# Perceiver block on one core: shifted-copy clearings, key powers, filter taps and the third level's masks in another order on VectorE and GpSimd

## The reference, cut to what matters

```python
q = _short_conv(hidden_states @ Wq.T, conv_q)          # 4 lags, then silu; the same for k and v_direct
beta = sigmoid(hidden_states @ Wb.T)
local_s, local_m, local_l = _fir(v_direct, fir_s), _fir(v_direct, fir_m), _fir(v_direct, fir_l)   # 3, 15, 63 lags
# delta rule: q, k normalised (k / sqrt(sum k*k)); kb = k * beta
A = where(tri_strict, -(kb @ k.T), 0);  T = solve_triangular(eye - A, eye)
...
probs = softmax(gate logits) * (1 - 5 eps) + eps
o = probs0*local_s + probs1*local_m + probs2*local_l + probs3*delta_out + probs4*v_direct
o = rmsnorm(o) @ Wo.T
```

## Time and profile before

| | us |
|---|---|
| median of 3 runs | 430.43 |
| lowest and highest of the runs | 428.21, 432.83 |
| the profiled execution, its own time | 433.92 |
| its span in the trace | 432.1 |
| mean granted TensorE clock of that execution | 0.987 of full |

### The profile page before, as it was taken

The page is one execution under the profiler, slowest core; times in us unless marked ns, Lnnn a source line. Parts: engine busy times, 40 slices in busy tenths (PEclk is TensorE's granted clock), DMA queues, the critical chain, the costliest instruction groups (busy, mean ns, idle before and its releaser), DMA issues.

```text
span 432.1 us, 8272 instructions
## 1 busy us (share of the span) xinstructions
PE 408.7 (95%) x3210; PEld 290.3 (67%) x3210; DVE 320.0 (74%) x583; ACT 189.0 (44%) x252; POOL 82.8 (19%) x81
## 2 busy tenths in 40 slices
PE   6999999999988989999999999999996999999994
PEld 5953458644434746687764688888884888888873
DVE  4742536697799999897598675855549699999966
ACT  1113322578652211023350445324426788887731
POOL 1100001000023800228741000368100000000065
PEclk9999999999999999999999999999997999999998
DMA  7999987947313540056000200287599889999645
GB/s 261 432 428 422 430 378 274 301 110 196 119 39 109 150 94 8 4 209 281 3 0 2 99 2 0 67 322 217 88 423 367 325 312 371 396 383 397 222 125 192
DMA packets 18227, 92.42 MB, mean 214 GB/s; under 512 B 3457, under 2 KB 5265, under 8 KB 11153
## 3 DMA queue, kind: packets, MB, share of 16 engines
q1 hardware_dynamic: 15168, 78.82, 49.6%
q10 hardware_dynamic: 1488, 8.93, 5.9%
q0 software_dynamic: 1536, 4.20, 3.0%
HBM read 82.25 MB, written 12.08 MB: 218 GB/s over the span
## 4 chain that ended last, share of the span: by engine, by line
PE 64%; DVE 13%; DMA 7%; POOL 6%; issue 5%; SPq 3%; ACT 1%; POOLq 0%; ACTq 0%; DVEq 0%
PE bank L984 22%; PE bank L797 8%; PE bank L721 5%; PE bank L747 5%; PE bank L626 3%; PE bank L603 3%; PE bank L650 3%; PE bank L576 2%; DVE part L1613 2%; POOL xs L522 2%; DMA early<-wffn_in 2%; SPq L376 2%; POOL info L526 2%; DVE ring L1613 2%; PE bank L771 2%
## 5 line engine op out<-in xcount | busy, mean ns | idle before, releaser
L1613 DVE SCALAR_TENSOR_TENSOR part<-ring,cols,part 128x504 f32<-128x504 f32 (+13 forms) x64 | 42.7, 725 | 0.2
L747 PE MATMUL bank<-xnT,ring 128*128 128x512 f32 (+1 forms) x96 | 37.7, 544 | 0.7 <-ACT xnT L1144 0.7
L797 PE MATMUL bank<-ring 64*64 64x64 f32 (+1 forms) x960 | 36.0, 224 | 2.4 <-POOL ring L484 1.3
L797 PEld LDWEIGHTS bank<-ring 64*64 64x64 f32 x960 | 31.8, 134 | 9.3 <-issue 5.7
L475 POOL TENSOR_TENSOR small<-small 128x1 f32<-128x1 f32 (+2 forms) x12 | 12.1, 1006 | 128.6 <-DVE small L1489 67.7
L721 PE MATMUL bank<-early,ring 128*32 128x512 f32 (+15 forms) x512 | 32.9, 396 | 0.5 <-DVE early L1632 0.5
L1613 DVE SCALAR_TENSOR_TENSOR ring<-bank,cols,ring 128x504 f32<-128x504 f32 (+2 forms) x36 | 26.3, 732 | 5.0 <-ACT ring L1207 4.1
L747 PEld LDWEIGHTS bank<-xnT,ring 128*128 128x128 f32 x96 | 17.6, 190 | 17.1 <-issue 15.3
L484 POOL TENSOR_TENSOR ring<-ring,consts 128x256 f32<-128x256 f32 x20 | 16.6, 857 | 46.8 <-DVE ring L1748 32.4
L984 PE MATMUL bank<-xe,hTs 128*128 128x512 f32 x72 | 20.6, 441 | 4.7 <-DVE hTs L2003 4.7
L1340 ACT ACTIVATE rows<-bank 128x512 f32<-128x512 f32 x19 | 11.3, 597 | 30.7 <-PE bank L984 30.7
(11 more groups left out here) (274 smaller groups left out, 936.5 us busy)
## 6 DMA issues: line engine op xcount, KB each, us to landing
early<-wffn_in SPq DMA_DIRECT2D x19, 1024.0 KB, 8.2
ring<-ctxT_in SPq DMA_DIRECT2D x4, 2048.0 KB, 20.1
ring<-ctx_in SPq DMA_DIRECT2D x4, 2048.0 KB, 34.5
raw1b<-wffn_in SPq DMA_DIRECT2D x7, 1024.0 KB
raw3b<-wffn_in SPq DMA_DIRECT2D x7, 1024.0 KB
raw2b<-wffn_in SPq DMA_DIRECT2D x6, 1024.0 KB, 8.2
ring<-firw_in SPq DMA_DIRECT2D x4, 1024.0 KB, 5.1
xs<-zeros_in ACTq DMA_DIRECT2D x1, 3840.0 KB, 13.9
```

The costliest lines, as they stand in the source:

```text
L747: last = pe.matmul(bank[QB[g % 3]][:, ts], wqkv[:, j, c, h * P:(h + 1) * P], xnT[:, c, ts], start=(c == 0), stop=(c == DC - 1))
L797: last = pe.matmul(dst[s, d], left[s, L * t:L * (t + 1)], right(s, t), start=True, stop=True)
L1613: return dve.scalar_tensor_tensor(out=d, in0=s, scalar=w, in1=d, op0=ALU.mult, op1=ALU.add)
```

## The change

No instruction is added or removed. Five things move:

- `clear_heads(0)` stands behind `convolve(H + 2)`, no longer in front of it and of tap 6; `clear_heads(1)` stands behind `gating_3()`, no longer in front of tap 7 and `convolve(2 * H)`.
- More taps stand early: 15 in place of 12 ahead of `want_powers(0)`, 17 in place of 14 ahead of `key_table()`, 20 in place of 18 ahead of `table_low`.
- In the first pair's ten steps the portions end at other taps: 8, 3, 4, 5, 4, 4, 3, 4, 4, 5 taps in place of 8, 3, 4, 5, 4, 4, 4, 5, 4, 5.
- `clear_heads(2)` stands in front of `query_table()`, no longer behind it.
- On GpSimd the third level's masks of the first pair (`level_masks(0, 2)`) stand in front of the queries' power, no longer behind it.

```diff
             level_masks(0, 1)
+            level_masks(0, 2)
             power(2 * NT + 2, 16, 16)
-            for l in range(2, NLV):
+            for l in range(3, NLV):
                 level_masks(0, l)
...
             gating_1()
+            fir_taps(6, 8)
+            convolve(H + 2)
             clear_heads(0)
-            fir_taps(6, 7)
-            convolve(H + 2)
             gating_2()
             convolve(H + 3)
-            clear_heads(1)
-            fir_taps(7, 8)
+            fir_taps(8, 10)
             convolve(2 * H)
             gating_3()
-            fir_taps(8, 12)
+            clear_heads(1)
+            fir_taps(10, 15)
             want_powers(0)
             convolve(2 * H + 1)
-            fir_taps(12, 14)
+            fir_taps(15, 17)
             key_table()
             convolve(2 * H + 2)
-            fir_taps(14, 18)
+            fir_taps(17, 20)
             table_low(0, ct_k, 3)
...
-            tap_ends = (18, 26, 29, 33, 38, 42, 46, 50, 55, 59, all_taps)
+            tap_ends = (20, 28, 31, 35, 40, 44, 48, 51, 55, 59, all_taps)
...
             for n in range(2 * NLV):
+                if n in (2, 5):
+                    clear_heads(2 + n // 5)
                 if n == 2:
                     query_table()
-                if n in (2, 5):
-                    clear_heads(2 + n // 5)
```

## The result

| | before | after |
|---|---|---|
| median of 22 runs each, us | 432.0 | 426.69 |
| lowest and highest | 428.21, 435.34 | 424.91, 431.26 |
| the profiled execution, its span | 433.92, 432.1 | 426.06, 424.2 |
| its mean granted TensorE clock | 0.987 | 0.998 |

The ratio is 0.9907, with a 95% interval of 0.9879 to 0.9934: the change gains 0.93%, 4.0 us of 432.0 (2.9 to 5.2). The forecast was 2.5 us. (The two medians lie 5.3 apart; since the times of both kernels gather round two values, as shown further down, a median jumps between them, and I go by the ratio.)

The account below looks back on a forecast made before the run. TensorE, busy 95% of the span, was taken as the bound, so only its waits could give. 1.38 + 0.35 + 0.85 - 0.41 + 0.20 + 0.17 = 2.5 us, median 430.43 to 427.9, range 424.8 to 431.3.

Parts of the forecast that it names:

- Part 1, clearings: Early stretch: later clearings 0 and 1, three more early taps remove TensorE's waits of 1.38 (key table) and 0.35 us.
- The clearings' DMAs do not move: Early stretch: the clearings' DMAs are bound by SyncE's issue, so their times stay as they were.
- Part 2, masks: Second level: two masks ahead of the queries' power slow fewer VectorE taps, gain 0.85; one hit in `mask_keys`, -0.41 us.
- the rule of a full block: `mask_keys`: an exclusive SBUF lock lets the moved masks block VectorE whole, the sum some 1.05 us less favourable.
- Part 3, "VectorE alone decides": Query powers to fourth level: VectorE sets the pace; TensorE waits about 1.0 for 0.81, leaves 2.37 us early.
- The 0.20 in front of `scale_query`: VectorE's idle moment there goes because the spread rows come in time, gain 0.20 us.
- The fifth level: Three and four taps in place of four and five remove TensorE's wait there, gain 0.17 us.
- TensorE runs through without waits: From 187 us on: no TensorE waits, all that follows hangs on the same chain, so the shift stays.
- sign of being wrong: Whole span: the prediction fails if the span differs by something other than the shift at 187 us.
- More: Rival: VectorE so far ahead that the levels' waits go whole; gain 4.4 us, time 426.0; chance 0.18.
- Little: Rival: holes only moved, key table late or masks hit `mask_keys` fully; gain 0.6 to 1.5, time 429.4; chance 0.16.
- Slower: Rival: another wait of about 4 us in the expert stage drops TensorE's clock; time 431.1; chance 0.09.

Follow-up runs that it names:

- 4: Changed kernel with all portions of taps put back as before; TensorE's stretch between the two marks took 89.65 us (changed kernel 89.41).
- 5: Changed kernel with clearings 0 and 1 put back in front of the convolutions; TensorE's stretch between the two marks took 93.25 us (changed kernel 89.41).
- experiment 2: Kernel before with only GpSimd's third-level masks moved ahead of the queries' power; TensorE's stretch between the two marks took 91.27 us (before 92.22).
- 6: Changed kernel with tap portions 7, 3, 4, 4, 4, 3, 6, 4, 4, 5; median 427.12 us, ratio to before 0.9872, stretch between the marks 88.18.
- 12: The kernel of 6 once more, on another chip; median 427.07 us, ratio to before 0.9867, stretch between the marks 88.07.
- kernel 1: Changed kernel with masks' order and clearing 2 put back, leaving the front alone; TensorE's stretch between the two marks took 90.19 us (before 92.22).
- experiment 11: Changed kernel unaltered, 12 runs on another chip; median 426.38 us, ratio to before 0.9916, stretch between the marks 89.40.
- 9: Kernel before with two of the 16 DMAs that build stack 1 split in halves; TensorE's stretch between the two marks took 95.03 us (before 92.22).

## Why the prediction was right, and where it was short

- **What bounds the kernel:** right. TensorE's own list didn't change (405.1 us busy after, 408.7 before with the half clock in it); what was gained is waits that went.
- **Part 1, clearings:** right, in each station. Request for the powers 0.8 us after VectorE gets there: 0.70. Wait of the table gone, 1.38, and that at the factors, 0.35. Alone, the front gave 2.03 where the sum has 1.73 + 0.17 = 1.90 for it. That it was the clearings and not the taps, which the prediction didn't separate, is shown by 4 and 5. "The clearings' DMAs do not move" holds for their place; what was missed is that their landing varies from one execution to the next.
- **Part 2, masks:** the forecast was 0.85 - 0.41 = 0.44; alone they gave 0.54. The three taps of the earlier trace rows fell from 3.23 to 2.45, the eight kept their 6.02, together 0.82 less; and one L1697 more took 0.84. The other 0.1 is idle time and overlap in front of the first L1748 (0.09 idle before, none after). The 1.05 us more that the rule of a full block would have cost did not come: one instruction was lengthened by 0.41. The turn-taking of that rule is in the rows all the same (experiment 2).
- **Part 3, "VectorE alone decides":** the waits that it names came as told (1.16 for "about 1.0" in the fourth level, the clearing's gone). The 0.20 in front of `scale_query` came too, but it belongs to clearing 2: the idle moment is 0.03 in all seven traces with that clearing early and the taps of the change or of before, and 0.20 to 0.25 in the five with it late. (With the portions of 6 and 12 it is 0.26 and 0.04.) The expectation of kernel 1 (89.8) had left it in the front, and taken the masks as 0.4 in place of 0.54; so kernel 1 stood at 90.19.
- **The size:** forecast 2.5, the stretch gave 2.8. Of the 0.3 some 0.14 are there from the key table and the factors on (1.87 for 1.73): probably a wait that goes gives back its own length and a little overlap of the matmuls around it, which no run shows by itself. The rest is in the masks' part: VectorE stands 2.50 earlier ahead of `scale_query`, 0.63 over the 1.87, where the forecast had 0.44. The fifth level gave 0.15 for 0.17.
- **Behind 187 us:** "TensorE runs through without waits" was wrong, against the earlier trace rows already. TensorE waits there for up to 4.5 us, and that part of the program took 238.9 to 244.9 us without being touched; so the spans can't show whether "the shift stays". The prediction's own sign of being wrong, a span that differs by more than the shift, did come: the profiled execution was forecast at 431.4 and took 426.06. Only S shows that the mechanism held.
- **The median:** the forecast of 427.9 lies near 426.69 partly by luck. It started from a median of 3 runs, 430.43, and 22 runs gave 432.0. And 2.8 is not 4.0, but lies at the edge of its interval. Two things lie between. The trace of before had an early landing of stack 0, its last issue 0.5 us ahead of the mean of the fourteen, and in the old order (1:1) that makes an average gain of some 3.3, an estimate; the 2.9 to 3.1 within a group is near it. For the rest, 17 of 22 runs of after fall in the quicker group, against 9 of 22 of before (8 of 12 against 7 of 17 in experiment 11). The two groups are 4 us apart, so such a shift is worth 1.0 to 1.5. Whether the change causes it, by the time at which the expert stage begins, or the draw of the runs does, stays open: no experiment moved the expert stage alone.
- **Rivals.** More (4.4) needed the levels' waits to vanish; they didn't, and only a new division of the taps (6) took most of them. Little fell with the waits at L739 and L772. Slower named a second wait of about 4 us that brings the clock down. It didn't come in the new order, but it stood nearer on the other side: in the old order a stack later by 1.3 us made a wait of 3.0 at the key table and a half clock behind it (9).

## What to carry to other kernels

An instruction that waits for a DMA belongs behind independent work that lasts until the DMA's latest landing, not its usual one: here that took 1.9 us out of the critical engine's stretch and made it the same in every execution. After such a move, look again where that engine still idles and shift the filling there: ten numbers in a list took another 1.2 us out of the stretch, which the whole times are too scattered to show. Where the end of a kernel scatters by more than an edit gains, measure between two marks of the trace that the edit doesn't touch, not by the spans.

## What the runs showed of the hardware

- Of the 16 equal DMA issues for stack 0 on SyncE, the second took 4.0 to 5.2 us and one of the 11th to 13th took 1.1 to 1.8, in all fourteen traces; the others took about 0.6 each (the third once 0.70 and once 1.06). Both long ones vary between executions of the same instructions.
- The granted clock does not answer to a wait's length alone: waits of 2.64 and 2.98 us had a half clock of 3.4 us behind them, one of 2.92 at the key table (5) and all up to 2.4 had none; of the waits of 3.8 to 4.5 us some had 3.4 and some 6.8.
- VectorE's instructions with two operands in SBUF took up to twice their time beside a GpSimd mask (L1697 0.84 for the 0.43 of the earlier trace rows), and the masks up to 1.15 for 0.73; they took turns, each ending a fixed 0.28, 0.50 or 0.59 us behind the other. Those with one operand in PSUM were not slowed (L1748 0.41), nor the mask beside them (0.73).
- Beside GpSimd's power the taps weren't slowed. The power took 3.3 us wholly beside taps and 2.9 beside a convolution and one or two taps; what makes the difference was not tested.
